# The last token tiles of a four-layer attention kernel one by one, and VectorE's small additions as reductions

## What is computed

```python
# L0: cross attention, 16 heads of 8, weights quantised to -g, 0, g
x = x + softmax(q @ k.T / sqrt(8)) @ v @ quant(Wo).T + bo
# L1: self attention, cross attention, feed-forward (512, gelu), each with a layer norm
x = layer_norm(x + mha(x, x, x, ..., tgt_mask))
x = layer_norm(x + mha(x, ctx, ctx, ..., src_mask))
x = layer_norm(x + gelu(x @ ff_w1 + ff_b1) @ ff_w2 + ff_b2)
# L2: gated sum with the mean of the context, layer norm
out = layer_norm(x + gate * softmax(coupling) * vision_proj)
# L3: RMS norm, rotary attention (16 query, 4 key heads of 64), RMS norm, SiLU feed-forward
hidden = hidden_states + attn @ Wo
x = rmsnorm(hidden, ln2_w)
return hidden + silu(x @ Wgate) * (x @ Wup) @ Wdown
```

## Time and profile before

| | |
|---|---|
| time, median of 3 runs (range) | 496.73 us (496.45 to 497.52) |
| time of the profiled execution | 496.65 us |
| its span, first to last instruction | 494.7 us |
| PE busy, PEld busy | 445.4 us (90%), 353.1 us (71%) |
| DVE, ACT, POOL busy | 381.2 us (77%), 299.3 us (60%), 273.8 us (55%) |
| mean granted share of PE's full clock | 0.99 |
| PE busy in 40 slices of the span (tenths) | 4698899999999999989989768999999999999876 |

### The profile page before, as it was taken

The page is one execution under the profiler, slowest core; times in us unless marked ns, Lnnn a source line. Parts: engine busy times, 40 slices in busy tenths (PEclk is TensorE's granted clock), DMA queues, the critical chain, the costliest instruction groups (busy, mean ns, idle before and its releaser), DMA issues.

```text
span 494.7 us, 16947 instructions
## 1 busy us (share of the span) xinstructions
PE 445.4 (90%) x6872; PEld 353.1 (71%) x6872; DVE 381.2 (77%) x918; ACT 299.3 (60%) x725; POOL 273.8 (55%) x332
## 2 busy tenths in 40 slices
PE   4698899999999999989989768999999999999876
PEld 4466666666666676679877656888888888878664
DVE  6699877688988888968889878877686876767632
ACT  2377676768676877666863655576656665544431
POOL 6464887579867787965644374454353535421210
PEclk9799999999999999999999999999999999999998
DMA  8960000000000000000000000000000000000000
GB/s 291 240 234 3 2 3 3 2 3 3 1 3 2 3 3 3 3 1 2 1 1 3 2 1 4 3 12 2 14 1 13 1 3 14 1 13 1 14 2 21
DMA packets 12421, 11.54 MB, mean 23 GB/s; under 512 B 5177, under 2 KB 10297, under 8 KB 12345
## 3 DMA queue, kind: packets, MB, share of 16 engines
q1 hardware_dynamic: 11624, 9.01, 6.7%
q10 hardware_dynamic: 720, 1.45, 0.8%
HBM read 9.42 MB, written 1.05 MB: 21 GB/s over the span
## 4 chain that ended last, share of the span: by engine, by line
PE 51%; DVE 24%; issue 14%; POOL 5%; ACT 4%; DMA 1%; DVEq 0%; POOLq 0%; ACTq 0%
DVE negm L1249 8%; PE ps L618 5%; DVE blocks L1240 5%; PE ps L634 4%; PE ps L656 4%; PE ps L448 4%; PE ps L734 4%; PE ps L466 3%; PE ps L532 2%; PE ps L545 2%; PE ps L611 2%; PE ps L626 2%; PE ps L496 2%; PE ps L664 2%; PE ps L408 2%
## 5 line engine op out<-in xcount | busy, mean ns | idle before, releaser
L1249 DVE TENSOR_REDUCE negm<-ps 128x8 bf16<-128x512 f32 x96 | 59.6, 683 | 24.9 <-PE ps L448 24.8
L833 ACT ACTIVATE p<-ps 128x512 f32<-128x512 f32 x96 | 54.7, 595 | 27.5 <-PE ps L456 26.4
L839 ACT ACTIVATE shared<-ps 128x512 f32<-128x512 f32 x96 | 57.0, 601 | 21.8 <-PE ps L466 20.4
L1742 POOL TENSOR_TENSOR wide<-wide,cv 128x1024 f32<-128x1024 f32 x24 | 45.5, 1896 | 32.8 <-ACT wide L823 32.8
L466 PE MATMUL ps<-cst,p 128*128 128x128 f32 x384 | 58.4, 276 | 0.4 <-ACT shared L839 0.4
L1795 POOL TENSOR_TENSOR probs<-p,rc 128x512 f32<-128x512 f32 x32 | 33.4, 1057 | 43.2 <-DVE rc L1535 43.1
L1669 POOL TENSOR_TENSOR rstd<-veps,neghalf 128x2 f32<-128x2 f32 x40 | 29.3, 732 | 46.4 <-DVE veps L1285 28.2
L466 PEld LDWEIGHTS ps<-cst,p 128*128 128x128 f32 x384 | 44.2, 141 | 11.5 <-issue 9.4
L1028 ACT ACTIVATE late<-ps 128x512 f32<-128x512 f32 x32 | 17.3, 594 | 34.3 <-PE ps L757 34.3
L618 PE MATMUL ps<-shared,wq 128*128 128x256 f32 x128 | 31.3, 386 | 5.2 <-ACT shared L976 3.4
L634 PE MATMUL ps<-wo,late 128*128 128x128 f32 x256 | 31.5, 276 | 4.0 <-ACT late L1028 3.8
(11 more groups left out here) (204 smaller groups left out, 1150.9 us busy)
## 6 DMA issues: line engine op xcount, KB each, us to landing
late<-in_mask_l SPq DMA_DIRECT2D x2, 512.0 KB, 11.0
result<-x_all SPq DMA_DIRECT2D x8, 128.0 KB, 1.8
x_all<-in_x_tok SPq DMA_DIRECT2D x1, 768.0 KB, 6.6
wide<-in_ctx_t SPq DMA_DIRECT2D x1, 768.0 KB, 8.1
rv<-in_rv ACTq DMA_DIRECT2D x1, 768.0 KB, 8.1
wa<-in_wa SPq DMA_DIRECT2D x1, 512.0 KB, 8.4
w<-in_w SPq DMA_DIRECT2D x2, 256.0 KB, 7.5
wq<-in_wq SPq DMA_DIRECT2D x1, 512.0 KB, 7.2
```

The costliest lines, as they stand in the source:

```text
L833: A_(p3[:, n % 3, :], ps[:, S_BANK[r], :], ACT.Exp, scale=SC8).then_inc(sm["act_exp"], 1)
L839: A_(pt[:, w % 2, r, :], pt_bank(RG * w + r), ACT.Copy).then_inc(sm["act_pt"], 1)
L1249: V.tensor_reduce(negm[:, n % 4, :], ps[:, S_BANK[r], :].rearrange("p (a k) -> p a k", k=S), AX.X, ALU.max, negate=True).then_inc(sm["dve_ ...
L1742: P.tensor_tensor(r_op[:, w % 2, :, :], k_t[:, w % 2, :].unsqueeze(1).to_broadcast([128, 4, GT]), head_masks.unsqueeze(2).to_broadcast([12 ...
```

## The change

It has three parts.

- **The end.** `ENDING` and the two rounds behind the last are replaced by `LAST` and `CLOSING`. Group 6 keeps its group-wise feed-forward, in another order. The norm (`n_in`), gate (`ng`), up (`nu`) and down (`nd`) projections of tiles 14 and 15 are made per tile, with all 512 columns of the gate in one bank. Those of tile 14 stand in the queues between the steps of tile 15's attention. SP stores the two tiles one by one.
- **The constants.** A third (or second) column beside the variances or sums holds the constant, written once at the start, and a `tensor_reduce` with add over the two columns takes the place of the `tensor_scalar`, 56 times in a run. The factor 1/128 moves into ACT's square. The factor -2 of L2's maxima becomes a negated sum of the value taken twice (8 more).
- **Two jobs moved.** `masks()` goes from `w == 4` to `w == 5`; the context's sums go from one instruction at `w == 2` to two halves at `w == 6` and `w == 7`, and ACT's reader from `w == 5` to `w == 8`.

```diff
-        mv = sb("mv", [128, 2, TG, 2])
+        mv = sb("mv", [128, 2, TG, 3])
...
-        ENDING = (
...
-        ROUNDS = range(NG + 2)
+        LAST = (("s0", 0), ("s1", 0), ("m_in", -1), ("pv0", -1), ("pv1", -1), ("mg0", -1), ("mu0", -1), ("out", -1),
+                ("mg1", -1), ("mu1", -1), ("t0", 0), ("t1", 0))
+        CLOSING = (("n_in", NT - 2), ("pv0", NT - 1), ("pv1", NT - 1), ("md", NG - 2), ("out", NT - 1), ("ng", NT - 2),
+                   ("nu", NT - 2), ("n_in", NT - 1), ("ng", NT - 1), ("nu", NT - 1), ("nd", NT - 2), ("nd", NT - 1))
+        ROUNDS = range(NG)
...
+            def token_gate_up(what, n):
+                pe.wait_ge(*released("n_in", n))
+                for f in range(FT):
+                    ins = mm(bank_of(what, n)[:, f * 128:f * 128 + 128], wg3[:, "gu".index(what[1]), f * 128:f * 128 + 128],
+                             hm_t[:, (NG - 1) % 2, n % 2 * 128:n % 2 * 128 + 128], start=True, stop=True, skip_group_check=True)
+                return ins
```

ACT's queue at the end:

```diff
+            def closing():
+                n = NT - 1
+                read("m_in", NG - 2)
+                evac_pv3(2 * n - 2)
+                evac_pv3(2 * n - 1)
+                exps3(2 * n)
+                exps3(2 * n + 1)
+                m_tanh(NG - 2, 0)
+                m_tanh(NG - 2, 1)
+                token_square(n - 1)
+                evac_t3(2 * n)
+                evac_t3(2 * n + 1)
+                token_rms(n - 1)
+                read("n_in", n - 1)
+                evac_pv3(2 * n)
+                evac_pv3(2 * n + 1)
+                token_square(n)
+                token_tanh(n - 1)
+                token_rms(n)
+                read("n_in", n)
+                token_tanh(n)
```

DVE's additions (one of the places) and the jobs moved:

```diff
-                V.tensor_scalar(veps[:, gs, :], mv[:, gs, :, 1], LN_EPS, None, ALU.add).then_inc(sm[s + "ve"], 1)
+                V.tensor_reduce(veps[:, gs, :], mv[:, gs, :, 1:3], AX.X, ALU.add).then_inc(sm[s + "ve"], 1)
...
-                if w == 2:
-                    dve.wait_ge(sm["ld_ctx0"], 16)
-                    dve.wait_ge(sm["ld_ctx"], 16)
-                    V.tensor_reduce(vpool[:, :], ctx_t[:, :].rearrange("p (b k) -> p b k", k=S), AX.X, ALU.add)\
-                        .then_inc(sm["v_sum"], 1)
-                if w == 4:
+                if w == 5:
                     masks()
+                if w in (6, 7):
+                    visual_sums(w - 6)
```

DVE's queue at the end:

```diff
+            def closing():
+                n = NT - 1
+                smax3(2 * n)
+                smax3(2 * n + 1)
+                sum3(2 * n)
+                sum3(2 * n + 1)
+                read("mg0", NG - 2)
+                read("mu0", NG - 2)
+                read("out", n - 1)
+                token_mean(n - 1)
+                read("mg1", NG - 2)
+                read("mu1", NG - 2)
+                read("md", NG - 2)
+                read("out", n)
+                token_mean(n)
+                read("ng", n - 1)
+                read("nu", n - 1)
+                read("ng", n)
+                read("nu", n)
+                read("nd", n - 1)
+                read("nd", n)
```

More of the change, by code:

```diff
@@ L353, in _ @@
             o_v = out.rearrange("(n p) d -> p n d", p=128)
-            for g in range(NG):
+            for g in range(NG - 1):
                 eng.wait_ge(*released("md", g))
@@ L658, in part_gate_up, with token_in, token_down @@
                 return ins
+            def token_in(n):
+                pe.wait_ge(sm["m_n"], n - NG + 2)
+                return nc.tensor.transpose(bank_of("n_in", n)[:, 0:128], hm[:, (NG - 1) % 2, n % 2, :], ident)
+            def token_gate_up(what, n):
[4 more added lines that the diff above has]
+                return ins
+            def token_down(n):
+                pe.wait_ge(*released("nu", n))
+                for i in range(FT):
+                    ins = mm(bank_of("nd", n)[:, 0:128], h3[:, i, n % 2 * 128:n % 2 * 128 + 128], wd3[:, i, :],
+                             start=(i == 0), stop=(i == FT - 1), skip_group_check=True)
+                return ins
             def part_down(g):
@@ L1170, in _ @@
             V.memset(ones[:, :], 1.0).then_inc(sm["ones_set"], 1)
+            for eps, tile in ((LN_EPS, mv[:, :, :, 2]), (LN_EPS, mv2[:, :, :, 2]), (RMS_EPS, ss3[:, :, :, 1]),
+                              (RMS_EPS, ssm[:, :, :, 1])):
+                V.memset(tile, eps).then_inc(sm["eps_set"], 1)
+            dve.wait_ge(sm["eps_set"], 4)
             dve.wait_ge(sm["ld_w0"], 16)
@@ L1453, in rms_mean @@
                 dve.wait_ge(sm["h_sq"], TG * g + TG)
-                V.tensor_scalar(ms3[:, g % 2, :], ss3[:, g % 2, :], 1.0 / D, RMS_EPS, ALU.mult, ALU.add)\
+                V.tensor_reduce(ms3[:, g % 2, :], ss3[:, g % 2, :, :], AX.X, ALU.add)\
                     .then_inc(sm["h_ms"], 1)
@@ L1458, in m_rms_mean @@
                 dve.wait_ge(sm["m_sq"], TG * g + TG)
-                V.tensor_scalar(msm[:, g % 2, :], ssm[:, g % 2, :], 1.0 / D, RMS_EPS, ALU.mult, ALU.add)\
+                V.tensor_reduce(msm[:, g % 2, :], ssm[:, g % 2, :, :], AX.X, ALU.add)\
                     .then_inc(sm["m_ms"], 1)
```

120 lines of the change are left out of this document (92 added, 28 removed), and 3 rows, old and new, of the table ENDING.

## The result

The changed kernel takes 491.92 us (median of 6 runs, 490.22 to 494.74) beside 496.76 us for the kernel before (496.45 to 497.52). The ratio is 0.9906, with a 95% interval of 0.9879 to 0.9934: faster by 0.9%, inside the forecast range, 1.9 us over the forecast of 490.0. The profiled execution took 491.76 us, its span is 489.7 us. Its runs scatter more than the six of before did, and with them the granted clock (over the 46 runs beside all kernels here the kernel before scatters as much, from 493.31 to 499.17): 490.22 us at a share of 0.997, 491.9 at 0.989 or 0.990, 494.74 at 0.978.

A forecast was written before the change was run, and what follows sets the result against it. PE holds half of the chain and DVE a quarter, so waits of PE or the chain count. -5.4 - 1.7 + 0.4 = -6.7 against 496.65 gave 489.95, forecast 490.0 us, range 487.8 to 492.8.

The forecast's parts named there:

- four steps shortened by half of 0.69 us: Last `out` to tile 15's gate: ACT steps handle one tile instead of two, 3.1 us instead of 3.98.
- that 4.6: Tile 15's gate to the last addition: gate, tanh, two products, down projection, one addition and five handovers, 4.6 us.
- rival 2: Around tile 15's norm at the end: the clock falls, up to +1.76 us, 491.9 us; chance 0.15.
- the 0.17 taken: Time taken for a reduction over two numbers that adds a constant: 0.17 us, that of the `tensor_scalar` itself.
- the upper bound of 0.412: Upper bound for a reduction over two numbers: 0.412 us, as over 256 numbers; would add 1.0 us in all.
- Rival 3: Constants: tiny reductions are slow (0.412 us each, 491.1 us) or wait for POOL as now (491.8 us); chance 0.08.
- rival 1: Masks at `w == 5`: not held up by POOL's product, jobs moved give -0.95, 488.7 us; chance 0.17.
- The forecast's +0.4: Jobs moved: masks wait for POOL's mask product, maxima of `w == 6` start at 68.1 instead of 67.70, +0.4 us.
- C: Jobs moved, masks to `w == 5` and halved context's sums to `w == 6` and `w == 7`: +0.4 us.
- A: The end, from tile 15's scores to the last addition, reordered per tile at full clock: -5.4 us.
- One sign of being wrong: The last `out` coming over 1 us later than the forecast of about 478.1.
- Rival 4: Product L1266 falls inside POOL's mask product in 11 rounds, 0.8 us each, 8.8 in all, 498.9 us; chance 0.02.

The follow-up runs named there:

- the one with the hole filled: The changed kernel with eight more matmuls on PE behind the scores of `w == 6`, before the wait for the maxima: 491.63 us, ratio 0.9905.
- the version with the wait at the start: Changed kernel, masks at `w == 6`, both sums at `w == 7`, POOL's first mask product waiting for DVE's norm of the second group: 489.17 us, ratio 0.9842.
- the one quoted above: Second profile of the changed kernel with masks at `w == 6` and both sums at `w == 7`; 488.06 us, ratio 0.9825.
- the fastest version: Changed kernel, masks at `w == 6`, sums at `w == 7`, POOL's first mask product waiting for DVE's norm, twelve filler matmuls in the third layer: 486.56 us, ratio 0.9788.

## Why the prediction was right

**The end (-5.4; measured -5.21).** Step by step: tile 15's transposes come 0.81 us earlier after its scores (forecast 0.8), and its last `out` ends 13.91 us behind them, 0.16 later than before (forecast 0.2). From there to tile 15's gate it is 3.01 us (forecast 3.1). Here luck helped: four steps shortened by half of 0.69 us, as the text puts its estimate, would have made 2.6. From the gate to the last addition it is 4.95 us (forecast 4.6). The terms of that 4.6 add up to 4.8, so half of the miss is the addition itself; for the rest, tanh followed 1.17 us behind the gate's start instead of 1.1, and the last down projection took 1.13 instead of 1.0. The clock was full at the end in all eleven profiles with the new one, as taken: rival 2 is out. The experiment with the old end confirmed the part as a whole. It also showed what the text said only in passing: 1.7 us of it is a clock fall that not every run of the kernel before has.

**The constants (-1.7; measured -1.67).** No small reduction waited; they took 145 to 163 ns, under the 0.17 taken and far from the upper bound of 0.412, and no round of the second phase has the 8.89 us of a wait. Rival 3 is out. The Trainium skill, page VectorE: DVE Perf Modes, section Rules for kernel authors, calls `tensor_reduce` the slowest operation and would restructure one on a hot path; for two numbers the runs decide the other way, 157 ns against 336 on average with its waits.

**The jobs moved (+0.4; measured +1.53).** This is the term that was mis-sized. The mechanism was right in each of its steps: the maxima of `w == 3` came 1.28 us earlier (forecast 1.36), the masks waited for POOL's product (rival 1 is out), the copy got in between, and the maxima of `w == 6` came 0.6 us late. The Trainium skill, page SBUF — State Buffer, section SBUF: two separate sides, has a VectorE operation in a mode with two ports, or with two inputs in SBUF, share a pair of ports with GpSimd; whichever starts first has it for its whole instruction, and the other blocks. The 1.50 us of a mask over 128 numbers agree with that, though no run here shows the mode. The forecast's +0.4 was -1.36 for the sums and +1.76 for the rest; measured were -1.28 and, with the half clock, +2.81. What failed is that the sum stopped there. It counted the delay on DVE and didn't ask what PE did meanwhile: it idled for 2.99 us, and half clock for 3.4 us behind that cost another 0.92. All five profiles with the masks at `w == 5` and the hole open had it; the one with the hole filled had not. I had read this very pattern in the earlier trace rows and used it for the end only.

**What came besides.** +2.06 us at 285 us and -1.46 at the start belong to the run and not to the change. The changed kernel's second profile has its first maximum at 19.94 us, 0.3 later than before, and only +1.07 in the third layer; the one with the old end and the second with the masks at `w == 6` took 314.75 us there, as the kernel before did (314.99). Of the 1.9 us over the forecast, C has 1.1, A 0.2, and these two 0.6. One sign of being wrong that the prediction names did come: the last `out` ended at 479.78 us and not at 478.1, 1.7 later, where 1 us was the limit. It is C's 1.1 and these two, not part A.

**Rival 4** did not come: L1347, the old L1266, takes 500 ns on average instead of 491, 0.2 us in all over 24.

## What to carry to other kernels

When a term says "this wait moves here", follow it to TensorE as well: a hole in PE costs its length only if it is on the path, but the half clock behind it can cost another microsecond. A job that uses what GpSimd uses belongs where GpSimd is idle and the engine that runs it too: with the same masks, `w == 2` to `w == 7` took 42.86 us where they stand at `w == 5`, 40.05 at `w == 4`, and 39.71 at `w == 6`. And note the granted clock beside every time: the two profiles of the kernel with the masks at `w == 6` differ by 3.0 us in the third layer, where one has two stretches at half clock and the other none.

## What the hardware showed that was not expected

- Work that computes nothing can pay: in the version with the wait at the start, 12 matmuls in PE's idle time took 2.6 us off, on the same chip (486.56 against 489.17). In the version without the wait the same 12 took off nothing (488.21 against 488.06), so it is not shown when it pays.
- A `tensor_scalar` from int32 over only 128 numbers was held up for the whole rest of POOL's product (1.50 us, and 0.21 without it). Between two such instructions that stand back to back on DVE, POOL's next instruction got in (65.97 to 66.36), and the second took 0.88 instead of 0.69 us.
- A stretch of PE at half pace at the start can make the start faster. In the changed kernel's first profile the projection at 10.43 us took 1.22 us, in the one quoted above 0.67:

```profile
10.43 1.22 PE L411 MATMUL ps<-in_t,wa 128*128 128x256 f32 x2 [0.66 <-ACT in_t L843]
```

  The first mask product came at 13.16, behind DVE's work, and the first maximum 1.46 us earlier than before. The one profile of the fastest version speaks for the product's start as what counts: there the projection took 0.70 us, the product was made to wait until 13.24, and the first maximum came at 18.38 us all the same.
